# Two layers on one core: GpSimd scales the queries before it adds the residual; PSUM is split into two convolution pairs and two banks each for turned and projected rows

## What is computed

```python
# layer 0: linear attention, 4 heads of 32
x = x + LN(linear_attention(GN(x)))      # q = softmax over d, k = softmax over tokens,
                                         # context = k v^T, out = (context q) w_out + b_out
# layer 1: gated 7x7 circular convolutions and 8 steps of a scan
gate_B = sigmoid(conv(GN(x), gB)); b = conv(GN(x), B) * gate_B
a = centre-tap map of A * sigmoid(conv(GN(x), gA))
h = scan of h <- c*h + v, 8 times, in log space
x = x + h @ W_out + b_out
```

## Time and profile before

| what | value |
|---|---|
| median of three runs | 6369.22 us |
| profiled execution | 6350.43 us, span 6348.7 us |
| TensorE matmuls | 5378.3 us busy (85%) |
| TensorE weight loads | 4931.3 us (78%) |
| VectorE | 4475.9 us (71%) |
| ScalarE | 4072.0 us (64%) |
| GpSimd | 4575.2 us (72%) |
| transfers | 1438.98 MB, mean 227 GB/s |
| mean granted TensorE clock | 0.950 of 2.4 GHz |

### The profile page before, as it was taken

How to read it: one execution, slowest core, us unless ns; L and a number is a source line. 1 busy time by engine, 2 the same in 40 slices (tenths; PEclk the granted TensorE clock), 3 DMA queues, 4 the chain that set the end, 5 groups by cost and what they waited for, 6 DMA issues and landing times. The chain is left out here.

```text
span 6348.7 us, 129369 instructions
## 1 busy us (share of the span) xinstructions
PE 5378.3 (85%) x49268; PEld 4931.3 (78%) x49268; DVE 4475.9 (71%) x5411; ACT 4072.0 (64%) x5384; POOL 4575.2 (72%) x3864
## 2 busy tenths in 40 slices
PE   6689999999999999999852688888888888888887
PEld 5578888888888888888752578887888788888887
DVE  7367777777777777777735977666667667676653
ACT  5677777777777777777512455565555555555554
POOL 0148888888888888888875977777777677777641
PEclk8899999999999999999955899999999999999999
DMA  5457777777777777777654599999999999999987
GB/s 129 128 161 229 229 235 229 226 232 230 230 228 233 229 229 230 232 229 216 182 159 119 146 256 264 256 260 260 262 263 266 258 262 271 265 266 257 255 244 212
DMA packets 1239102, 1438.98 MB, mean 227 GB/s; under 512 B 142960, under 2 KB 1025396, under 8 KB 1238516
## 3 DMA queue, kind: packets, MB, share of 16 engines
q1 hardware_dynamic: 1238516, 1431.07, 79.3%
HBM read 999.09 MB, written 431.64 MB: 225 GB/s over the span
## 5 line engine op out<-in xcount | busy, mean ns | idle before, releaser
L1296 PE MATMUL psC<-wide,xhl 128*128 128x256 bf16 x6144 | 1050.5, 282 | 50.8 <-DMA wide<-toeplitz_wide 38.0
L1226 POOL TENSOR_TENSOR stage<-stage,nrow 128x1024 f32<-128x1024 f32 x240 | 620.7, 2586 | 370.6 <-DMA stage<-x_by_block_row 348.3
L1293 PE MATMUL psC<-wide,xhl 128*128 128x192 bf16 x6144 | 873.6, 252 | 0.0
L1243 POOL COPY down<-xhl 48x448 f32<-48x448 f32 x512 | 507.1, 990 | 454.7 <-PE psC L1302 355.0
L1387 ACT ACTIVATE xhl<-psC 128x512 f32<-128x512 f32 x512 | 303.1, 598 | 652.2 <-PE psC L1302 650.6
L1494 DVE SCALAR_TENSOR_TENSOR xhl<-xhl,psC 128x512 f32<-128x512 f32 x512 | 347.1, 680 | 453.8 <-ACT xhl L1387 453.5
L1293 PEld LDWEIGHTS psC<-wide,xhl 128*128 128x128 bf16 x6144 | 644.6, 116 | 17.6
L1302 PE MATMUL psC<-narrow,down 128*128 128x96 bf16 x6144 | 532.9, 211 | 146.4 <-POOL down L1246 90.9
L1402 ACT ACTIVATE hT<-psH 128x512 f32<-128x512 f32 x512 | 304.8, 595 | 543.0 <-PE psH L1338 542.8
L852 POOL TENSOR_TENSOR y<-y,grow 128x1024 f32<-128x1024 f32 x256 | 606.0, 2367 | 61.9 <-DVE y L686 61.9
L1296 PEld LDWEIGHTS psC<-wide,xhl 128*128 128x128 bf16 x6144 | 595.9, 116 | 64.6 <-issue 51.6
(11 more groups left out here) (178 smaller groups left out, 14120.0 us busy)
## 6 DMA issues: line engine op xcount, KB each, us to landing
wide<-toeplitz_wide SPq DMA_DIRECT2D x1024, 140.0 KB, 5.7
xa<-in_x SPq DMA_DIRECT2D x256, 512.0 KB, 4.7
xb<-in_x SPq DMA_DIRECT2D x256, 512.0 KB, 3.9
xc<-in_x SPq DMA_DIRECT2D x256, 512.0 KB, 4.5
x_rows<-xc SPq DMA_DIRECT2D x256, 512.0 KB
res<-x_rows SPq DMA_DIRECT2D x256, 512.0 KB, 8.8
out<-res SPq DMA_DIRECT2D x256, 512.0 KB, 8.0
stage<-x_by_block_row SPq DMA_DIRECT2D x225, 512.0 KB, 8.7
```

Of the source, the lines that this page charges most:

```text
L1226: nc.gpsimd.tensor_tensor(v, v, nrow[:, 0:1, :].to_broadcast([P, NP_, C]), ALU.mult).then_inc(s_scaled, 1)
L1243: nc.gpsimd.tensor_copy(dst[lo, :, :, 0:last], src[lo, :, 0:NQ, CW:])
L1293: nc.tensor.matmul(dst[:, :, :, 2:], lhs, tab[:, :, 32 + part * 12:44 + part * 12], start=False, stop=False)
L1296: nc.tensor.matmul(dst, lhs, tab[:, :, part * 16:part * 16 + 16], start=(n == 0), stop=False)
```

## The change

In layer0, GpSimd's scaling of the queries is put ahead of the residual's addition. In layer1, psC has two pairs instead of three, and the two banks that this frees go to a second psH and a second psO, used in turn. conv_first waits for the product of two blocks before, turn(t) for the copy of row t-2, project(t) for the addition of row t-2. The small windows are transposed into the four row banks.

```diff
                         nc.gpsimd.tensor_tensor(y[:], y[:], grow[:].unsqueeze(1).to_broadcast([P, TPC, C]), ALU.mult
                                                 ).then_inc(s_yg, 1)
-                        pool.wait_ge(s_yg, gc - 1)
-                        pool.wait_ge(s_xc[m % 4], owner * (4 * NCH) + m // 4 * 16 + 16)
-                        v = xc[m % 4][:, :, 0:C]
-                        nc.gpsimd.tensor_tensor(v, v, y[:], ALU.add).then_inc(s_x1, 1)
                     if live(img, gb - 1):
                         pool.wait_ge(s_qinv, gb)
...
                         nc.gpsimd.tensor_tensor(qv, qv, iv, ALU.mult).then_inc(s_qn, 1)
+                    if live(img, gc - 2):
+                        pool.wait_ge(s_yg, gc - 1)
+                        pool.wait_ge(s_xc[m % 4], owner * (4 * NCH) + m // 4 * 16 + 16)
+                        v = xc[m % 4][:, :, 0:C]
+                        nc.gpsimd.tensor_tensor(v, v, y[:], ALU.add).then_inc(s_x1, 1)
...
-    WR, NR, DR, CR = 3, 2, 2, 3
+    WR, NR, DR, CR, OR = 3, 2, 2, 2, 2
...
-        psH = ps("psH", [C, HS, P])
-        psO = ps("psO", [P, HS * C])
+        psH = [ps(f"psH{k}", [C, HS, P]) for k in range(OR)]
+        psO = [ps(f"psO{k}", [P, HS * C]) for k in range(OR)]
...
-            return (psH[:], psO[:].rearrange("p (s c) -> p s c", c=C),
-                    psC[2][:, 0:2].rearrange("p c v m -> p (c v) m"),
-                    psC[2][:, 2:4].rearrange("p c v m -> p (c v) m"))[k]
+            return (psH[0][:], psO[0][:].rearrange("p (s c) -> p s c", c=C),
+                    psH[1][:], psO[1][:].rearrange("p (s c) -> p s c", c=C))[k]
...
-                count = img * NBLK + wide_before(blk) + 1
+                count = img * NBLK + blk - CR + 1
                 if known(count):
                     pe.wait_ge(s_prod, count)
...
-                count = oi * HR + t
+                count = oi * HR + t - OR + 1
                 if known(count):
                     pe.wait_ge(ht_evac, count)
...
-                    mm = nc.tensor.transpose(psH[:, s, :], hv[:, :, t * HS + s], ident[:])
+                    mm = nc.tensor.transpose(psH[t % OR][:, s, :], hv[:, :, t * HS + s], ident[:])
...
-                count = oi * HR + t
+                count = oi * HR + t - OR + 1
                 if known(count):
                     pe.wait_ge(s_added, count)
-                nc.tensor.matmul(psO[:].rearrange("p (s c) -> p s c", c=C), ones3[:],
+                nc.tensor.matmul(psO[t % OR][:].rearrange("p (s c) -> p s c", c=C), ones3[:],
...
-                    mm = nc.tensor.matmul(psO[:, s * C:(s + 1) * C], hT[:, t % 2, s * P:(s + 1) * P], w[:],
+                    mm = nc.tensor.matmul(psO[t % OR][:, s * C:(s + 1) * C], hT[:, t % 2, s * P:(s + 1) * P], w[:],
```

More of the change, by code:

```diff
@@ L1401, in evacuate @@
                     act.wait_ge(o_ready, count)
-                nc.scalar.activation(hT[:, t % 2, :], psH[:].rearrange("p s m -> p (s m)"), ACT.Copy,
+                nc.scalar.activation(hT[:, t % 2, :], psH[t % OR][:].rearrange("p s m -> p (s m)"), ACT.Copy,
                                      bias=A_FREE * H_EPS, scale=A_FREE).then_inc(ht_evac, 1)
@@ L1554, in add @@
                 part = res[:, k, (t % 2) * HS * C:(t % 2 + 1) * HS * C]
-                nc.vector.tensor_tensor(part, psO[:], part, ALU.add).then_inc(s_added, 1)
+                nc.vector.tensor_tensor(part, psO[t % OR][:], part, ALU.add).then_inc(s_added, 1)
             def image(img, par, has_conv, has_out, has_stage):
```

## The result

| what | before | after |
|---|---|---|
| median | 6371.78 us (4 runs) | 6296.68 us (4 runs, 6282.89 to 6310.05) |
| ratio | | 0.9875, 95% interval 0.9851 to 0.9899 |
| profiled execution, span | 6350.43, 6348.7 us | 6310.05, 6308.3 us |

The change makes the kernel 75 us faster; the forecast was 103. The profiled execution of before lies 21 us under its median and that of after 13 us over its own, so the spans differ by only 40. Profiles of kernels with the same first layer start the second one within 5 us of each other, while executions of one kernel differ by 10 to 50 us in the whole. So the first layer is read from the profiles, the size of the second from the medians.

A forecast was written before the change was run, and what follows sets the result against it. TensorE was nearly full in the first layer, transfers all but full mid-image in the second. Terms -32, -56 and -15 made -103 us: 6350.43 to 6247, plus 18.8 for the median, 6266; range 6190 to 6350.

The forecast's parts named there:

- rival B: Second layer: transfers give back everything in the middle of an image, first layer and tail gains stay; 6322 us, chance 0.18.
- the last two images: End of the second layer: waits for additions go where transfers have room; -15 us, bounds 5 and 20.
- Queries ahead of the addition: First layer: scaling first shortens regular steps by 0.22 us, the first five steps lose some; -32 us in all.
- this is partly given back in the steps behind; I keep +0.4 an image: First layer, first five steps of an image: +0.85 us seen in one, mostly recovered later, leaving +0.4 an image.
- Rival D: First layer: the late sum binds, each of the first five steps loses 0.85 us; 6366 us, no change, chance 0.08.
- Two banks each: Second layer, full images: second psH and psO remove up to 199.4 us of waits, transfers allow 4 an image; -56 us.
- a share of 1.02 may rise to about 1.05, 3% of the 132 us in which it is full: Second layer, middle of an image: transfers can speed up only slightly, which sizes the gain at 4 us an image.
- the sign that the prediction set itself: Full image of the second layer: 170.5 us expected; 160 would mean no transfer limit, 174 a middle that gains nothing.
- Two PSUM pairs: Second layer: first matmuls wait 2.9 us for the product at blocks 31 and 3; hidden, so cost 0.
- The covers: Second layer: existing waits hide the new ones, 3.5 us for tables behind block 31, 3.9 for the softplus at block 3.
- A: Second layer: the full DMA share is no limit, so all the bank waits become gain; 6118 us, chance 0.12.
- C: Second layer, conv_first: two pairs become the ring, waits only change name and 5.8 us an image is added; 6424, chance 0.12.

The follow-up runs named there:

- e0_after: The changed kernel run once more, on the same chip as the other follow-up runs: 6306.89 us, ratio 0.9894 to the kernel before.
- e15_pso_only: Kernel before with two psC pairs and a second psO, psH kept at one and one bank unused: 6308.32 us, ratio 0.9882.
- e6_late_scale: Changed kernel with GpSimd's scaling of a stage one slot later in the second layer: 6303.33 us, ratio 0.9883 to the kernel before.
- e14_pairs_only: Kernel before with two psC pairs, psH and psO kept at one bank each, two banks unused: 6377.18 us, ratio 0.9992.
- e9_half_tables_new: Changed kernel loading only the lower half of each wide-table band, about a sixth fewer bytes: 6151.07 us, ratio 0.9653 to the kernel before.

## Why the prediction was right, and where not

Faster was right, and the measured 6296.68 lies in the range. The sum was -103 us, measured are -75 (-67 by the ratio of e0_after). The time lies about halfway between the forecast (6266) and rival B (6322), and it is that near because the last two images gave 9 us more than taken while the other two terms gave less.

**Queries ahead of the addition** (-32; measured -9). The chain was read rightly: the addition closes it, the Gram waits for it, GpSimd idles for qinv, and steps 5 to 15 give 2.4 us an image, as 11 x 0.22 said. The step that failed is "this is partly given back in the steps behind; I keep +0.4 an image". It is 2.3: +1.01, +0.19, +0.73, +0.13 and +0.24 in the five steps. The earlier trace rows had shown +0.85 in one; nothing had shown it given back. The step with the latest qinv (3.5 us after the gain) was not looked up: one row each of the five steps would have priced most of it. Half a microsecond of step 0, VectorE's slower L765 beside the late addition, no row of before could show. Rival D had this mechanism, but priced each of the five at 0.85, where they cost 0.46 on average, and took the other 11 for worthless.

**Two banks each** (-56 in the middle; measured about -42). The times say -75 + 9 + 24 = -42; the profiles say less: an image takes 174.6, 175.5 and 175.8 us in three kernels with the old tiles, 174.0, 173.7, 172.5 and 172.0 in four with the new ones. The means are 2.25 us apart, 32 us in 14 images (e15_pso_only has 171.9, e6_late_scale, with its other order, 175.0). So a full image gained 2 to 3 us where 4 were taken. Half tables bear out that the banks held the kernel before and that the transfers hold it now. But the step that gave the size failed: "a share of 1.02 may rise to about 1.05, 3% of the 132 us in which it is full". Over rows 0 to 31 the share rose from 1.02 to 1.03 while the rate stayed at 278 GB/s, and that stretch got no shorter (133.8 us, then 135.3). The 2 to 3 us come from the 41 us behind it, with a share near 0.75, where the forecast took nothing; that they are near 4 is luck. By the sign that the prediction set itself, an image of 174 us, the middle is rival B's, and B was right for the stretch in which the share is full. The forecast also spread the gain over both banks. The runs put all of it on psO: where the releaser of L1348 was named as the addition or the correction of hT, 153.8 us, the bank was the cause; the 45.6 us on ScalarE's copy were worth nothing, and without a second psO taking them away goes with 23 us more.

**The last two images** (-15, bounds 5 and 20; measured -24, and -18 in the profile of e0_after). The step that failed is the sum over waits. With one bank, project, addition and next project form a ring of 2.14 us a row; TensorE alone needs 1.55. An estimate is 0.59 x 31 = 18 us for the 31 waits of the earlier trace rows, where each showed 0.44 to 0.5; from the first to the last of the 32 projections behind the blocks it took 67.9 us and takes 51.7, 16 less (56.5 in e0_after). Some 6 us more lie in the blocks of image 15, where the DMA share rose too (0.83 to 0.88 in the first 136 us).

**Two PSUM pairs** (0; measured 0, e14_pairs_only 0.9992). The covers held, and the places were nearly right. Counted by block in images 1 to 14, e14_pairs_only has these waits at block 31 in all 14 images (38.5 us, 2.7 each, where 2.9 was taken) and at block 3 in four. The kernel after has 14 at block 31, six at block 3 and two elsewhere. With half tables they come 55 times, 30 of them at other blocks.

**Rivals.** A (no DMA limit, 6118) falls with full tables; e9_half_tables_new comes near its image, 162.5 us against 174.6 - 14.2 = 160.4. The Trainium skill, Perfetto Trace Analysis, section Matmul Optimizations, advises to use all eight PSUM banks. Both kernels use all eight, and e15_pso_only has the whole gain with seven; what counts here is which tile has them. B (6322) had the middle at nothing; it gave some 32 to 42 us, outside the stretch with the full share. C fell with e14_pairs_only. D was half right, above.

**Left open.** Why a second psH alone makes the kernel 23 us slower. Its twelve executions had mean granted clocks of 0.943 to 0.946 of full speed, those of e14_pairs_only 0.946 to 0.950, those of the kernel before beside it 0.945 to 0.949. Its longest wait at L1347 was 5.7 us against 4.0, and all of TensorE's waits add up to 8 us more than in e14_pairs_only. As an estimate, 0.003 of 6400 us is 19 us of TensorE's work at full clock, most of what is missing. Whether the clock is the cause or follows from the waits, no run tells. The same goes for the gain: all executions of the kernels with a second psO had 0.949 to 0.957, all others 0.943 to 0.951. What part of the 65 us came through the clock is not shown. More room for the narrow tables, the natural next step, was not tried, since the memory on chip is full.

## What to carry to other kernels

Two limits that nearly coincide look like one in a list of waits: the sum over TensorE's waits (361 and 351 us here) tells more than the rows that vanish, and taking a sixth of the bytes away from both kernels tells which limit each has. A wait is worth most where the next limit has room, so split the repeating unit where the DMA share changes and price each wait by the part in which it lies. Where operations are exchanged on a queue, price every kind of step that the loop has, above all those in which the operand now awaited is late, and use the new order only where it wins. When a buffer is doubled, the gain of a row is the ring's period less the engine's own work, which can be more than the wait listed, as long as nothing else binds there.

## What the runs showed of the hardware

The DMA share follows the kind of transfer, not the bytes alone: from 1500 to 3000 us the kernel after moved 229 GB/s at a share of 0.77, while in the second layer 220 GB/s took 0.82 and 235 took 0.88. In the second layer the rate for each unit of share stayed near 270 GB/s (220/0.82, 235/0.88, 263/0.97). A share near 1 in the second layer thus stands for 270 to 300 GB/s. There a cut in bytes took 10 us from the rows of an image once the banks no longer bound, as e9_half_tables_new shows.

VectorE's addition L765 (128 x 512 elements) took 0.68 or 0.69 us in 211 of its 240 instructions in the kernel after. In the other 29 GpSimd's addition L864 ran beside it for a part of its time, and it took 0.85 to 1.78 us.
